# The small operations behind an autocorrelation search, rewritten on VectorE

## What is computed

```python
# 1. low-rank adapters, chosen per sample
y = einsum('bnr,bor->bno', einsum('bni,bri->bnr', x, B[ids]), A[ids])
# 2. autocorrelation over the positions, the 6 best delays, and a weighted sum of y rolled by them
corr = irfft(rfft(y) * conj(rfft(y)))
weights, delay = top_k(corr, 6)
x = x + sum_k softmax(weights)[k] * roll(y, -delay[k])
# 3. a 64x64 mix of the channels, chosen per sample
z = einsum('bct,bcd->bdt', x, W[cond])
# 4. a dense layer with bias, plus two of eight low-rank experts by a router
h = z @ W_base.T + b_base + experts(z, router(z)) * 2
# 5. the residual
out = x + h          # x from step 2
```

## Time and profile before

| what | value |
|---|---|
| median of 3 runs | 867.25 us (866.4 to 868.05) |
| the profiled execution | 867.77 us, its span 865.8 us |
| busy: PE, DVE, POOL, ACT | 782.6, 655.7, 531.1, 328.9 us |
| shares of the chain that ended last | PE 51%, POOL 18%, DVE 13%, issue 6%, ACT 5%, DMA 4% |
| POOL idle before its gathers (L1085) | 202.5 us in 160 gathers |
| rp (L942), DVE, 128x2 | 32 times, mean 1817 ns |

### The profile page before, as it was taken

One profiled execution on the slowest core, in us unless ns is written; L12 is line 12 of the kernel. 1 busy time (PEld: TensorE's weight loads), 2 busy tenths in 40 slices (PEclk: granted clock), 3 DMA queues, 4 the chain that ended last, 5 costly groups with the idle time before them and its releaser, 6 DMA issues.

```text
span 865.8 us, 14359 instructions
## 1 busy us (share of the span) xinstructions
PE 782.6 (90%) x4808; PEld 650.5 (75%) x4808; DVE 655.7 (76%) x1362; ACT 328.9 (38%) x616; POOL 531.1 (61%) x464
## 2 busy tenths in 40 slices
PE   5655699899998999899998999899998999999897
PEld 4544588778877888778786888778886888878686
DVE  1335588987888787987878888888878888888852
ACT  4453334334443434334443335334443333333211
POOL 0326576846686666856486676856696676666621
PEclk9756699999999999999999999999999999999999
DMA  8477678776877688776877698786878687786621
GB/s 269 139 226 222 193 252 256 243 242 196 268 239 243 211 259 256 241 238 196 252 243 238 210 279 240 225 231 219 259 242 240 216 251 246 240 242 197 192 76 48
DMA packets 65804, 194.26 MB, mean 224 GB/s; under 512 B 13596, under 2 KB 23228, under 8 KB 62532
## 3 DMA queue, kind: packets, MB, share of 16 engines
q0 software_dynamic: 23040, 83.90, 32.4%
q1 hardware_dynamic: 30932, 70.80, 28.4%
q10 hardware_dynamic: 11760, 38.66, 11.6%
HBM read 117.82 MB, written 50.33 MB: 194 GB/s over the span
## 4 chain that ended last, share of the span: by engine, by line
PE 51%; POOL 18%; DVE 13%; issue 6%; ACT 5%; DMA 4%; SPq 1%; ACTq 1%; POOLq 0%; DVEq 0%
PE o_ps L437 25%; POOL turn L1108 5%; PE h_ps L556 5%; PE x_ps L461 4%; PE c_ps L437 4%; POOL rolled L1085 4%; PE x_ps L545 3%; POOL row L1071 3%; DVE row L917 3%; POOL eo L1111 3%; POOL eo L1112 3%; DMA y_d<-y 2%; PE t_ps L514 2%; PE t_ps L491 2%; ACT eo_hi L791 2%
## 5 line engine op out<-in xcount | busy, mean ns | idle before, releaser
L1085 POOL DMA_INDIRECT rolled<-y_d,off x160 | 209.1, 1307 | 202.5 <-DVE mirror L885 97.5
L917 DVE SCALAR_TENSOR_TENSOR row<-rolled,weight,row 128x1024 f32<-128x1024 f32 x160 | 221.2, 1383 | 12.5 <-DMA rolled<-y_d,off 6.6
L437 PE MATMUL o_ps<-wt_hi,x_hi 128*128 128x512 f32 x512 | 219.9, 429 | 0.0
L437 PE MATMUL o_ps<-wt_hi,x_lo 128*128 128x512 f32 x512 | 203.3, 397 | 0.0
L437 PE MATMUL o_ps<-wt_lo,x_hi 128*128 128x512 f32 x512 | 203.0, 396 | 0.0
L437 PEld LDWEIGHTS o_ps<-wt_hi,x_hi 128*128 128x128 f32 x512 | 97.5, 190 | 22.0 <-issue 4.6
L437 PEld LDWEIGHTS o_ps<-wt_hi,x_lo 128*128 128x128 f32 x512 | 96.4, 188 | 23.3
L437 PEld LDWEIGHTS o_ps<-wt_lo,x_hi 128*128 128x128 f32 x512 | 97.1, 190 | 15.5
L1071 POOL TENSOR_TENSOR row<-row,bias 128x1024 f32<-128x1024 f32 x32 | 78.0, 2437 | 17.8 <-PE x_ps L545 17.2
L731 ACT ACTIVATE turn<-t_ps 128x512 f32<-128x512 f32 x64 | 34.9, 596 | 132.4 <-PE t_ps L491 132.4
L1108 POOL TENSOR_TENSOR turn<-turn 128x256 f32<-128x256 f32 x64 | 74.3, 1180 | 2.6
(11 more groups left out here) (129 smaller groups left out, 1464.8 us busy)
## 6 DMA issues: line engine op xcount, KB each, us to landing
y_d<-y ACTq DMA_DIRECT2D x64, 512.0 KB
row<-in_x SPq DMA_DIRECT2D x32, 512.0 KB, 7.4
adapter<-g_hi SPq DMA_DIRECT2D x64, 256.0 KB, 5.4
out<-row SPq DMA_DIRECT2D x32, 512.0 KB, 6.0
adapter<-g_lo SPq DMA_DIRECT2D x32, 256.0 KB, 5.7
r<-in_L_cond_A SPq DMA_DIRECT2D x64, 64.0 KB, 4.0
r<-in_L_cond_B SPq DMA_DIRECT2D x56, 64.0 KB
rolled<-in_L_ffn_W_base SPq DMA_DIRECT2D x5, 512.0 KB, 6.1
```

The costliest lines, as they stand in the source:

```text
L437: last = pe.matmul(dst, a, b, start=start and n == 0, stop=stop and n == len(todo) - 1)
L917: dve.scalar_tensor_tensor(rows[:, :], from_buffer[:, :], weight[:, n:n + 1], rows[:, :], ALU.mult, ALU.add).then_inc(sum_step, 1)
L1085: pool.indirect_dma_start(out=rolled[at % RB][:, :], out_offset=None, in_=y2_d[u], in_offset=bass.IndirectOffsetOnAxis(ap=off[s % 2][:, n: ...
```

## The change

The thirteen small instructions become eleven. The first offset is computed without the delay as a step between: twice the position plus the row's base, then the correction for even or odd positions. The mirrored delays are no longer computed from the delay: a new constant column, `rowmirror`, minus the offset gives the mirrored offset. The test for the middle (`not_mid`) is not an instruction of its own: a scalar_tensor_tensor compares the position and multiplies in one (`part_v`, `part`). Where an instruction needs the result of one before it, independent ones now stand between them, and the wait is for the count of the needed one. The last offsets stand behind the wait for `y_free`. `top_step` rises 13 times a tile instead of 15, and POOL waits for count 12 instead of 11 before the fourth gather.

```diff
...
@@ -98,7 +98,8 @@
     small = np.zeros((P, SMALL))
     small[:, :P] = np.eye(P)
     small[:, P] = np.arange(P) * 2 * L + 1
-    small[:, P + 1:TALL] = np.arange(E)
+    small[:, P + 1] = np.arange(P) * 4 * L + L
+    small[:, P + 2:TALL] = np.arange(E)
     small[:, TALL:TALL + P] = (np.arange(P)[:, None] % TR // R) == (np.arange(P)[None, :] // C)
     small[:, TALL + P:] = np.tile(np.eye(TR), (BG, 3))
     return {"dft": dft.astype(np.float32), "back": back.astype(np.float32),
...
@@ -171,10 +174,10 @@
         val = sb("val", [P, 8])
         idx = sb("idx", [P, 8], U32)
         is_mid = sb("is_mid", [P, 2])
-        not_mid = sb("not_mid", [P, 2])
         part = sb("part", [P, 2])
         in_even = sb("in_even", [P, 3])
-        delay = sb("delay", [P, NSEL])
+        part_v = sb("part_v", [P, 2])
+        delay = sb("delay", [P, 3])
         mirror = sb("mirror", [P, 3])
         off = [sb(f"off{k}", [P, NSEL], U32) for k in range(2)]
         neg_max = sb("neg_max", [P, 1])
@@ -296,7 +299,7 @@
         biased = sem("biased")
         fold_step = sem("fold_step")
         blk = ctx.enter_context(nc.Block())
-        TOPS, RS, FS = 15, 9, 6
+        TOPS, RS, FS = 13, 9, 6
         SUMS = NSEL + 1
 
 
@@ -877,21 +880,26 @@
                 dve.wait_ge(top_step, n[0])
                 step(dve.max_index(idx[:, :], val[:, :], corr))
 
-                step(dve.tensor_scalar(in_even[:, :], idx[:, 0:3], float(Q), 1.0 - H, ALU.is_ge, ALU.mult))
-                step(dve.scalar_tensor_tensor(delay[:, 0:3], idx[:, 0:3], 2.0, in_even[:, :], ALU.mult, ALU.add))
-                step(dve.tensor_scalar(off[k][:, 0:3], delay[:, 0:3], rowbase, None, ALU.add), False)
+                step(dve.tensor_scalar(in_even[:, :], idx[:, 0:3], float(Q), 1.0 - H, ALU.is_ge, ALU.mult), False)
+                step(dve.tensor_scalar(delay[:, :], idx[:, 0:3], 2.0, rowbase, ALU.mult, ALU.add))
+                step(dve.tensor_tensor(off[k][:, 0:3], delay[:, :], in_even[:, :], ALU.add), False)
+                off_step = n[0]
                 step(dve.tensor_scalar(is_mid[:, :], idx[:, 0:2], float(H - 1), None, ALU.is_equal), False)
-                step(dve.tensor_scalar(not_mid[:, :], idx[:, 0:2], float(H - 1), None, ALU.not_equal), False)
-                step(dve.tensor_scalar(mirror[:, :], delay[:, 0:3], -1.0, float(L - 2), ALU.mult, ALU.add))
-                step(dve.tensor_tensor(part[:, :], mirror[:, 0:2], not_mid[:, :], ALU.mult))
-                step(dve.scalar_tensor_tensor(delay[:, 3:5], is_mid[:, :], mirror[:, 2:3], part[:, :],
-                                              ALU.mult, ALU.add))
-                step(dve.tensor_scalar(off[k][:, 3:5], delay[:, 3:5], rowbase, None, ALU.add), False)
-                step(dve.tensor_tensor(part[:, :], val[:, 0:2], not_mid[:, :], ALU.mult))
+                step(dve.scalar_tensor_tensor(part_v[:, :], idx[:, 0:2], float(H - 1), val[:, 0:2],
+                                              ALU.not_equal, ALU.mult), False)
+                dve.wait_ge(top_step, off_step)
+                step(dve.tensor_scalar(mirror[:, :], off[k][:, 0:3], -1.0, rowmirror, ALU.mult, ALU.add), False)
+                mirror_step = n[0]
                 dve.wait_ge(y_free, s + 1)
                 step(dve.tensor_scalar(neg_max[:, :], val[:, 0:1], corr0[k][:, :], -1.0, ALU.max, ALU.mult), False)
-
-                step(dve.scalar_tensor_tensor(val[:, 3:5], is_mid[:, :], val[:, 2:3], part[:, :],
+                dve.wait_ge(top_step, mirror_step)
+                step(dve.scalar_tensor_tensor(part[:, :], idx[:, 0:2], float(H - 1), mirror[:, 0:2],
+                                              ALU.not_equal, ALU.mult), False)
+                part_step = n[0]
+                step(dve.scalar_tensor_tensor(val[:, 3:5], is_mid[:, :], val[:, 2:3], part_v[:, :],
+                                              ALU.mult, ALU.add), False)
+                dve.wait_ge(top_step, part_step)
+                step(dve.scalar_tensor_tensor(off[k][:, 3:5], is_mid[:, :], mirror[:, 2:3], part[:, :],
                                               ALU.mult, ALU.add), False)
                 step(dve.tensor_copy(val[:, 5:6], corr0[k][:, :]), False)
 
@@ -1078,7 +1086,7 @@
                         pool.wait_ge(top_step, TOPS * s + 5)
                         pool.wait_ge(y_saved, 32 * (s + 1))
                     if n == 3:
-                        pool.wait_ge(top_step, TOPS * s + 11)
+                        pool.wait_ge(top_step, TOPS * s + 12)
                     if at >= RB:
                         added, of = (at - RB) // NSEL, (at - RB) % NSEL
                         pool.wait_ge(sum_step, SUMS * added + of + 2)
```

More of the change, by code:

```diff
@@ L49 @@
 LORA_SCALE = 2.0
-TALL = P + 1 + E
+TALL = P + 2 + E
 SMALL = TALL + P + STK
@@ L119, in build @@
         rowbase = const[:, P:P + 1]
-        iota8 = const[:, P + 1:TALL]
+        rowmirror = const[:, P + 1:P + 2]
+        iota8 = const[:, P + 2:TALL]
         mask = const[:, TALL:TALL + P]
@@ L139, in tiles @@
     ident, mask, repeat, rowbase, iota8 = v["ident"], v["mask"], v["repeat"], v["rowbase"], v["iota8"]
+    rowmirror = v["rowmirror"]
     ids, bias, dft_m = v["ids"], v["bias"], v["dft_m"]
```

## The result

The changed kernel took 880.65 us (median of six runs from 876.75 to 896.07), the kernel before 866.25 in the same comparison. So the kernel is slower, by 14.4 us by the medians and some 12.5 by the ratio, where 10 were forecast (877, range 858 to 886). The profiled execution took 880.75, with a span of 878.6, so 12.8 more span than the profiled one of before.

A forecast was written before the change was run, and what follows sets the result against it. Except in spectrum slots, the chain to POOL's power sums, ACT's eo_hi, PE's correlation and the search sets a slot's length. 11.5 + 5.4 - 4.2 = 12.7, less 2.5, gave +10: 877 us, range 858 to 886.

The forecast's parts named there:

- the trap: DVE's weights, asked during POOL's third gather, are held until the bias addition behind it ends; chance 0.56, +10 us.
- The search: DVE's small instructions that find a tile's best delays get 0.95 us shorter, bounds 0.5 to 1.1.
- The weights do not move, POOL does: Third slot: weights stay at 7.79 us after its start; third gather moves from 8.16 to 7.2, bias to 8.15.
- The hold: Weights wait for the bias addition and end at 10.57 us after the slot's start; 2.8 us in 13 to 17 slots.
- spectrum slots: Six slots that PE fills without a gap: no loss, period stays 25.5 us.
- The rule of the lock: DVE and POOL share a port pair; the instruction that starts first has it for its whole length, the other blocks.
- The strict reading: The weights, first in line, would go when the gather ends: a wait of 0.35 us, not 2.8.
- Fold slots: Six slots where POOL still folds the next group's adapters: each gains 0.70 us, at most 0.95; 4.2 in all.
- Third and fourth slots and their like: Seventeen slots go to 24.1 us: third kind loses 11.5 us in all, fourth kind 5.4.
- The 2.5: Taken off the loss for four or five slots whose second addition waits for its rows, making the second gather short.
- 12.7: Forecast loss in us over all slots: 11.5 plus 5.4 less 4.2, before 2.5 is taken off.
- the threshold: Weights are caught if the third gather starts before some 7.45 us into the slot, from 0.7 us of saving on.

The follow-up runs named there:

- e1: The changed kernel, with POOL's bias addition also waiting until the slot's softmax weights are written: 856.84 us, against 867.34 for the kernel before.
- e5: The changed kernel, with the weights computed by a tensor_tensor instead of a tensor_scalar with a per-partition operand: 879.82 us, against 868.01 for the kernel before.
- e12: The kernel before, with two idle MAX8 over 340 columns ahead of the weights' reciprocal: 947.87 us, against 866.22 without them.
- e11: The changed kernel, bias addition ahead of the gathers, but in fold slots behind them and waiting for the weights: 849.53 us, against 866.22 for the kernel before.
- e2: The kernel before, with POOL's bias addition also waiting for the slot's weights: 866.87 us, against 867.34 without the wait.
- e9: The changed kernel, with one idle MAX8 over 360 columns on DVE behind the search: 891.12 us, against 866.22 for the kernel before.
- e4: The changed kernel, with eight idle one-column memsets on DVE behind the search: 889.32 us, against 867.34 for the kernel before.
- e10: The changed kernel, with one idle MAX8 over 128 columns on DVE behind the search: 891.91 us, against 866.22 for the kernel before.

## Why the prediction was right

The bet was on the trap, and its mechanism came as described. The closeness of the total is partly luck, as the sum at the end of the list shows.

- *The search* was to be 0.95 shorter: it is 1.00 (1.22 for 1.2 to 1.3). The spacings of the earlier trace rows carried over.
- *The weights do not move, POOL does:* weights at 7.79, third gather at 7.16 (7.2 forecast), 0.94 long, bias at 8.11 (8.15).
- *The hold:* the weights are out at 10.57 (10.57), right behind the bias. e1 shows that this is the cause, e5 that the form is not, e12 that the change is not needed for it. It holds the weights for over 2 us in 22 slots, not in 13 to 17; six of these are spectrum slots, where it costs nothing.
- *The rule of the lock.* In e1 the weights wait 0.30, to the gather's end, and in the changed kernel 2.78, through the gather and the bias. That a running instruction keeps the port pair to its end, as the Trainium skill has it (SBUF — State Buffer, Who interferes with whom), agrees with both. It does not fit the first part of a gather: in e11's rows add_y asks 0.27 into one and takes its usual 1.28. The strict reading, that the waiting instruction is next, would give 0.3 in both if the order of asking is the order of starts in the trace, and so read it fails: POOL's bias starts 0.3 us after the weights had asked, and went first. But the starts may hide when POOL's next instruction gets in line. Over all profiled runs, with the bias ready behind the gather, 27 add_y asked up to 0.24 into the gather passed and all 33 asked from 0.27 on were held; of the weights all 35 asked up to 0.16 passed and all 128 from 0.30 on were held. With no bias there (11 add_y, asked 0.27 to 0.33 into the gather), or one that the weights had released less than 0.1 us before (3 of e1 and e2, asked 0.30 to 0.67), all took 1.28 or 1.29. That looks as if a ready bias gets in line some 0.25 us after the gather's start (an estimate from these bounds), and the first in line then goes first. No row shows that moment itself, so this stays an inference.
- *Fold slots* were to gain 0.70 each: they gain 0.60 to 0.95, 4.1 in all (4.2). There the bias still holds rp (2.73).
- *Spectrum slots* stay at 25.54, though the weights are held there too.
- *Third and fourth slots and their like* (17): 19.9 more in the profiled run, where 16.9 less 2.5 was forecast. Had the three slots of the next two points been as long as their kind, it would be 14.6. The 2.5 was for slots with a late landing and a short second gather (0.94). There are five: four take 23.4 to 23.9, the fifth is that of the landing below.
- *Not forecast, the clock.* PE now waits 1.75 us for s_t in each such slot. (The chain calls it issue; it ends 0.1 after s_t is written.) In two third slots (25.69 and 25.63) its clock fell behind that wait, which cost 1.6 and 1.5.
- *Not forecast, a landing that sets the trap for add_y:* in the fourth slot from 627.03 the second addition starts at 7.33, after 2.71 of waiting for its rows. So the third gather starts as late as 8.88 and the weights pass, but add_y asks 0.30 into the gather and is held for 4.13 (rows below). ACT's squares start at 14.86 instead of 13.4, the clock falls too, and the slot takes 26.25: 2.2 more than the 24.0 of its kind.
- *Not forecast, start and end.* The first search starts 1.0 later, the two slots behind it are 1.6 shorter, and what follows the last search is 2.4 shorter: -3.0, priced at nothing.

So 12.7 - 2.5 + 3.1 + 2.2 - 3.0 = 12.5, against 12.8 measured. Terms that nobody had forecast add 5.3 and take off 3.0, and so cancel in part: that is luck. What failed is smaller but worth more elsewhere: the threshold. The prediction put it at a third gather ahead of 7.45 and asked of the weights alone. e9 passed that line and was as slow, as add_y was caught. Both must be asked ahead of the gather's start or close behind it, or the bias must not stand ready there.

The slot from 627.03 of the changed kernel, DVE and POOL:

```profile
635.96 0.23 DVE L912 TENSOR_SCALAR weight<-ex,ex_inv 128x6 f32<-128x6 f32 x1
636.22 4.13 DVE L917 SCALAR_TENSOR_TENSOR row<-y,weight,row 128x1024 f32<-128x1024 f32 x1
...
635.92 0.94 POOL L1093 DMA_INDIRECT rolled<-y_d,off  x1 [3.05 <-DVE row L925]
```

The chain below is that of the changed kernel, in order of time (start us, us, what), in the slot from 305.42 and then in the one from 602.91.

```profile
315.95 1.75 issue
317.71 1.57 PE t_ps L517 x8
319.28 1.73 PE x_ps L446 x8
...
613.44 1.75 issue
615.20 1.08 PE t_ps L517 x8
616.27 0.90 PE x_ps L446 x8
```

Windows of the same two stretches, and between them one from the slot from 627.03: busy us of PE, PEld, DVE, ACT, POOL (instructions), then granted clock, DMA share, GB/s.

```profile
316.00:323.50 7.50, 5.79 (x27) 5.33 (x28) 5.64 (x10) 2.36 (x3) 2.86 (x5) 0.77 0.61 207
642.50:645.70 3.20, 3.20 (x10) 2.42 (x9) 2.16 (x2) 1.26 (x2) 2.57 (x4) 0.50 0.13 49
613.50:621.00 7.50, 5.80 (x34) 5.06 (x35) 6.06 (x12) 3.14 (x5) 3.37 (x5) 1.00 0.65 225
```

In the first and the last row it is the same wait and the same work: eight matmuls of L446 take 1.73 in the one slot and 0.90 in the other. That is the lower of the two levels (1.2 against 2.4 GHz) for a while. Why one slot fell and others did not stays open. The profiles of e4, e9 and e10 show it in 8, 4 and 6 slots, that of the changed kernel in 3, and these three medians lie 9 to 11 us above the changed kernel's.

## What to carry to other kernels

Work taken off an engine that is not the bound shifts when its neighbours' work starts. Ask what that work releases (here POOL's gathers), what stands ready behind it in the same queue, and which short instruction of the critical chain now asks in the middle of it; the price is the length of what runs and of what is queued behind it, not of the short instruction. The cure is to put the long instruction where the other engine needs nothing of what they share, or to gate it behind the short one; busy time shows neither.

## What was not expected of the hardware

- Whether a VectorE instruction is held depends on when it asks and on what stands ready behind the gather. With the bias ready, add_y passed up to 0.24 us behind the gather's start and was always held from 0.27 on (4.0 to 4.1, its own time included); the weights passed up to 0.16 and were always held from 0.30 on (2.5 to 3.1). With none there, add_y was never held, up to 0.33. The weights took 0.23 when asked at 0.41 (e2, one case, its bias waiting for them), and when asked 0.55 to 0.66 behind the start of a 0.94 us gather they waited for its end, 0.28 to 0.39 in all.
- Eight one-column memsets in a row cost 0.12 us together, where the search's own small instructions are 0.07 to 0.13 apart; MAX8 over 360 and 128 columns moved what follows by 0.44 and 0.20.
- A 1.75 us wait of PE was in some slots followed by a granted clock of 0.77 over 7.5 us, and in others by an unchanged 1.00.
